# The place of eight scatter DMAs on the GpSimd queue of a two-layer transformer kernel

## The reference

```python
x = L0_attn_x                                    # (8, 256, 256)
h = _layernorm(x) * (1 + ca) + sa
x = x + ga * _L0_attn_ref(h, ...)                # 16 heads, causal softmax
h = _layernorm(x) * (1 + cb) + sb
x = x + gb * _L0_ffn_ref(h, ...)                 # 8 experts, top 2, and a shared one
h = _layernorm(x) * (1 + ca) + sa                # the second layer's ca, sa, ...
x = x + ga * _L1_attn_ref(h, ...)                # linear attention with a memory
h = _layernorm(x) * (1 + cb) + sb
x = x + gb * _L1_ffn_ref(h, ...)                 # 16 experts, top 4

# _L1_ffn_ref
t = xf * rsqrt(mean(xf * xf) + EPS) * norm_w
vals, idx = top_k(t @ gate_w.T + gate_b, 4)
G = zeros((M, E)).at[arange(M)[:, None], idx].set(softmax(vals))
h = einsum('mh,eoh->emo', t, w1) + b1[:, None, :]
act = a * sigmoid(ALPHA * a) * (b + 1.0)         # a, b: even and odd rows of h, clipped
y = einsum('emi,edi->emd', act, w2) + b2[:, None, :]
delta = einsum('me,emd->md', G, y)
return x + delta
```

## Time and profile before

| | |
|---|---|
| median of 3 runs | 1023.02 us |
| lowest, highest | 1021.14, 1023.75 us |
| the profiled execution's own time | 1023.02 us |
| its span, first to last instruction | 1021.0 us |
| busy: PE, DVE, ACT, POOL | 971.4, 715.6, 673.2, 426.9 us |
| mean granted TensorE clock | 0.984 |

### The profile page before, as it was taken

How to read it: one execution, slowest core, us unless ns; L and a number is a source line. 1 busy time by engine, 2 the same in 40 slices (tenths; PEclk the granted TensorE clock), 3 DMA queues, 4 the chain that set the end, 5 groups by cost and what they waited for, 6 DMA issues and landing times.

```text
span 1021.0 us, 20557 instructions
## 1 busy us (share of the span) xinstructions
PE 971.4 (95%) x6068; PEld 820.3 (80%) x6074; DVE 715.6 (70%) x2498; ACT 673.2 (66%) x1944; POOL 426.9 (42%) x445
## 2 busy tenths in 40 slices
PE   8999999999999999999999999999898799999990
PEld 5669878987977887888888788887677589999990
DVE  4464657766777677778777757784887678888880
ACT  3657768578668667857766866794746366777750
POOL 2322422331362254146145316424166556556563
PEclk9999999999999999999999999999999899999995
DMA  9926992999599220021021004337167799989964
GB/s 317 306 85 225 377 376 98 318 377 348 196 336 376 104 85 33 1 95 44 1 81 58 1 2 167 96 141 255 27 168 184 202 250 221 230 215 217 234 146 82
DMA packets 94380, 180.52 MB, mean 177 GB/s; under 512 B 9965, under 2 KB 29101, under 8 KB 93757
## 3 DMA queue, kind: packets, MB, share of 16 engines
q1 hardware_dynamic: 74459, 148.85, 43.9%
q0 software_dynamic: 18464, 30.01, 12.8%
q10 hardware_dynamic: 1346, 0.36, 0.2%
HBM read 77.42 MB, written 107.99 MB: 182 GB/s over the span
## 4 chain that ended last, share of the span: by engine, by line
PE 85%; DMA 4%; DVE 4%; issue 2%; POOL 2%; SPq 1%; ACT 1%; DVEq 0%; ACTq 0%; POOLq 0%
PE bank L1163 12%; PE bank L1129 11%; PE bank L1101 10%; PE bank L1184 6%; PE bank L1119 5%; PE bank L1091 5%; PE bank L1080 4%; PE bank L1050 3%; PE bank L1090 3%; PE bank L1120 3%; PE bank L1110 3%; PE bank L959 2%; PE bank L950 2%; PE bank L1032 2%; DMA RA<-in_L_attn_Wo 2%
## 5 line engine op out<-in xcount | busy, mean ns | idle before, releaser
L1978 POOL TENSOR_TENSOR RB<-RB 128x512 f32<-128x512 f32 x64 | 67.0, 1047 | 259.9 <-DVE RB L1764 259.7
L1163 PE MATMUL bank<-RB 128*128 128x128 f32 x1264 | 158.1, 277 | 2.8 <-DVE BC L1874 0.7
L1163 PEld LDWEIGHTS bank<-RB 128*128 128x128 f32 x1264 | 150.3, 193 | 6.2 <-ACT RB L1453 1.5
L1446 ACT ACTIVATE RB<-RA,nw 128x512 f32 x158 | 105.5, 714 | 48.4 <-issue 25.7
L1129 PE MATMUL bank<-RA,RB 128*128 128x256 f32 x512 | 133.0, 382 | 2.0 <-ACT RB L1347 2.0
L1101 PE MATMUL bank<-RA 128*128 128x256 f32 x512 | 121.3, 380 | 0.0
L1101 PEld LDWEIGHTS bank<-RA 128*128 128x128 f32 x512 | 95.0, 190 | 15.0 <-issue 3.3
L1129 PEld LDWEIGHTS bank<-RA,RB 128*128 128x128 f32 x512 | 91.2, 190 | 15.9 <-issue 3.0
L1954 POOL TENSOR_TENSOR qs<-qs,half 128x4 f32<-128x4 f32 x64 | 65.7, 1027 | 62.4 <-DVE qs L1773 49.3
L1184 PE MATMUL bank<-RB,BC 128*128 128x256 f32 x316 | 83.6, 388 | 1.7 <-DVE BC L1887 1.3
L1347 ACT ACTIVATE RB<-bank 128x256 f32<-128x256 f32 x128 | 48.6, 380 | 47.8 <-PE bank L1120 46.7
(11 more groups left out here) (253 smaller groups left out, 2383.2 us busy)
## 6 DMA issues: line engine op xcount, KB each, us to landing
xsD<-BC SPq DMA_DIRECT2D x17, 4232.0 KB, 32.9
RB<-in_w2b SPq DMA_DIRECT2D x79, 256.0 KB
RB<-xsD SPq DMA_DIRECT2D x61, 264.5 KB, 3.7
BC<-modD SPq DMA_DIRECT2D x16, 512.0 KB, 3.8
RA<-in_w SPq DMA_DIRECT2D x10, 512.0 KB
X<-xsD SPq DMA_DIRECT2D x18, 264.5 KB
RA<-in_L_attn_Wq SPq DMA_DIRECT2D x2, 1024.0 KB, 12.0
RA<-in_L_attn_Wo SPq DMA_DIRECT2D x1, 2048.0 KB, 18.5
```

Of the source, the lines that this page charges most:

```text
L1163: m = pe.matmul(ps[:, 128 * j:128 * j + 128], WS[:, n % 2, c, 128 * j:128 * j + 128], XT[:, n % 2, c * 128:c * 128 + 128], start=(c == 0), ...
L1446: m = act.activation(WS[:, n % 2, c, :], W1[:, bass.ds(r, 1), c, :].rearrange("p a n -> p (a n)"), ACT.Copy, scale=nw[:, c:c + 1])
L1978: pool.tensor_tensor(sq, qrow, qrow, ALU.mult).then_inc(mine("q_sq", p), 1)
```

## The change

The table `SENDS` and the method `put_behind` go. In their place stands a method `spread`, called with four `f_send` of sequence 6 and four numbers. It takes them out of the list and puts each behind a POOL stage counted from the last other `f_send` of sequence 6. The sequence 5's sends are in no call any more, and stay where the planner puts them.

```diff
-    def put_behind(self, moves):
-        for k, anchor in moves:
+    def spread(self, keys, every):
+        for k in keys:
             self.order.remove(k)
-            self.order.insert(self.order.index(anchor) + 1, k)
+        pool = [i for i, (stage, *key) in enumerate(self.order) if ENGINE[stage][0] == "POOL" and self.engine({"do": (stage, *key)}) == "POOL"]
+        last = max(i for i in pool if self.order[i][0] == "f_send" and self.order[i][2] == keys[0][2])
+        behind = [i for i in pool if i > last]
+        for n, k in reversed(list(enumerate(keys))):
+            self.order.insert(behind[every[n]] + 1, k)
...
-    (("f_send", 1, 5, 0, 3), ("ln_rs", 2, 6)),
...
-    (("f_send", 1, 5, 1, 3), ("f_send", 1, 5, 1, 2)),
-)
+SPREAD = 0, 1, 4, 5
...
-    p.put_behind(SENDS)
+    p.spread([("f_send", 1, 6, i, k) for i, k in ((1, 0), (1, 1), (1, 2), (1, 3))], SPREAD)
```

More of the change, by code:

```diff
@@ L192, in do @@
     return {"do": (stage, *key), **how}
[L195 to L199, removed]
-    (("f_send", 1, 5, 0, 3), ("ln_rs", 2, 6)),
-    (("f_send", 1, 5, 1, 0), ("f_gain", 5)),
-    (("f_send", 1, 5, 1, 1), ("f_x", 5)),
-    (("f_send", 1, 5, 1, 2), ("ln_rs", 1, 7)),
-    (("f_send", 1, 5, 1, 3), ("f_send", 1, 5, 1, 2)),
-)
+SPREAD = 0, 1, 4, 5
 W1_PARTS = (
```

## The result

The changed kernel took 1026.16 us (median of 19 runs, 1022.88 to 1029.08), the kernel before in the same sessions 1020.79 (19 runs, 1019.24 to 1023.75). The ratio is 1.0052, with a 95% interval of 1.0043 to 1.0060: slower by 5.4 us, where 1023.0 and no difference were forecast, and outside the range.

What follows compares the result with a forecast made beforehand. PE was taken as the bound, busy 971.4 of 1021.0 us. Terms 0 + 0 + 0 on the profiled execution's 1023.02 us gave 1023.0, range 1020.8 to 1025.6.

Steps and rivals of the forecast that it cites:

- The sends' pace: POOL, sequence 5: sends follow each other every 1.27 us, up to 1.36 beside DVE; last before `ln_rs(2, 6)` ends at 695.90.
- The step costs nothing as long as PE's earlier work covers it: Four more sends before `ln_rs(2, 6)` end it 1.53 us later, but PE's transposes still get data in time: cost 0.
- The term that the sum put at nothing: Cost of moving four sends ahead of `ln_rs(2, 6)` on POOL: taken as 0, upper end 0.6 us.
- the 0.6 taken as upper end: If each of the four sends took 1.54 us, data would reach PE at 698.85, 0.60 us late.
- the 0.48 us of cover: Slack left between `ln_x(2, 6)` data reaching PE at 697.77 and PE's transposes (L939) starting at 698.25.
- The port: Rival: the port shared with DVE holds sends from 692.4 on; transposes late 1.7 to 2.3 us, 1024.7 to 1025.3; chance 0.06.
- the full engines: Rival: full DMA engines hold the four sends; PE's data 6.7 us late, time 1029.7; chance 0.04.
- `f_gain(5)`, `f_x(5)`, the last weight loads: On POOL 1.5 and 0.4 us later; SP waits for both, but last weight loads still leave near 703.6: cost 0.
- the 2.6 us of cover on SP: SP's slack after `store(5)`, ending about 700.6, before the last two weight loads go out from 703.59.
- The sends that leave: Later sequence 5 sends on POOL, at 709.54, 711.08 and behind `f_x(5)`, go: gain taken as 0, bound 0.63 us.
- 0.06 for slower: Chance of slower beyond 0.3% (3.07 us): 0.04 for full engines, 0.02 for a port holding longer than priced.
- theory B: From the experiments, not the forecast: a long unbroken row of indirect sends on POOL keeps PE's completions from DVE and ACT.

Runs made afterwards that it cites:

- the first two experiments: Changed kernel with three weight loads held until sequence 5's sends landed: 1028.15 us, ratio 1.0056; changed kernel with those sends cut to 16 numbers a row: 1026.62 us, 1.0040.
- the run with six powers: Kernel before, sends in old places, with six small powers on POOL between the third send and `ln_rs(2, 6)`: 1025.03 us, ratio 1.0021.

## Why the prediction was wrong

**The sends' pace: right.** Seven at 1.26 to 1.28 us steps; the last ended at 694.84, 695.87 in before's time, against 695.90 forecast.

**"The step costs nothing as long as PE's earlier work covers it": this step failed.** It priced the sends only by how late they make POOL, and took it that PE, DVE and ACT go on meanwhile. On a chip with the stall they don't: from about 5 us behind the first send (691.25 against 686.17; by 3.4 us in sequence 7's row of before, 801.87 against 798.47), what PE has finished isn't taken up by DVE and ACT, which stand idle 3.75 and 4.15 us. The term that the sum put at nothing is 3.25 us of idle PE and 1.5 us for the clock at 0.50, 4.75 of the 5.0 us between the spans. The lateness itself, on the chip without the stall, is worth 0.77 us of idle time, beyond the 0.6 taken as upper end; the 0.48 us of cover counted on an `ln_x` of 0.74.

**The port and the full engines.** Both have the right sign and neither the mechanism. Sends never stood still; the first two experiments take the loads and the data away and the stall stays. The evidence against them was sequence 7's train, read for the pace of the sends alone. Its neighbours on ACT, DVE and PE in the same 10 us held the stall: 4.62, 3.61 and 4.60 us of idle time in the very rows' time. That one omission made a 5 us loss look like no change.

**`f_gain(5)`, `f_x(5)`, the last weight loads: not tested as priced.** Everything moved with PE: `bc(1, 7)` to 700.16, `store(5)` to 701.33, the last loads to 707.24 instead of 703.59. With 1.03 of shift the loads are 4.68 late, as much as PE; the 2.6 us of cover on SP held.

**The sends that leave: right.** No gain shows.

**The chances.** 0.06 for slower was too little for an order that had one example of itself in the trace, unread.

What stays open: by what means the row delays completions. The matmuls' starts are on time and the consumers are late, and the trace can't say whether the results or their news come late. The Trainium skill, "Perfetto Trace Analysis" (section "Tensor Engine Instruction (MATMUL, LD_WEIGHTS)"), says that TensorE's end in a profile is an estimate, and that the acknowledgement from PSUM and the update of the semaphore come behind it. That fits ends of 691.25 and 691.89 with consumers at 694.68 and 696.09, and no row here sees the step between. Open too: why one of three chips has no stall, how long a row may be (DVE was late by 0.84 us in a row of three, by 0.71 and 2.29 in rows of four), and the 2 us of the run with six powers. That theory B is the cause is shown by the length of the row, by the pauses and by the move to sequence 3; that it is the indirect form, only together with its longer time on POOL.

## What to carry to other kernels

Where a change makes a pattern longer that the kernel already has somewhere, read all engines at that place of the trace, not only the one that runs the pattern; a wait for "remote" on a core that shares with no other is something to explain first. Keep rows of indirect DMAs on POOL short beside TensorE work: here rows of two and three, with 1 us between, no longer made PE stand still for its results. Put other work of POOL between them that waits for nothing, even useless work, but not ahead of a step that PE waits for. Compare on more than one chip before believing "no difference".

## What the runs showed that I had not expected

- A row of seven indirect DMAs of 128 rows leaves DVE and ACT idle for 3.7 and 4.2 us in front of TensorE's results, whatever the bytes (16 or 529 numbers a row: 4.17 and 4.15 us on ACT). Five: 2.6 and 1.6. Three: none, but for a result that came only after the row. A pause of 2 us, or two of 1 us, shortens it so far that PE no longer waits for it.
- It showed on two chips and in the first traces, and never on the third: sequence 3's row cost 0.49% on one and 0.07% (interval with 0) on another.
- The last wait of the stall ends 1.2 to 1.6 us behind the end of the row's last send (ACT at sequence 5: 1.22 and 1.25; DVE at sequence 3: 542.23 against 540.66).
- A plain DMA of the same bytes holds POOL for 0.56 us (3.92 for seven), an indirect one for 1.27.
- Behind 3.25 us without work, TensorE's granted clock was 0.50 for the next 3 us.
- DVE's pair of `TENSOR_SCALAR` took 0.74 us beside a send, and in other traces 2.48 or 2.95, ending 0.15 us behind POOL's own arithmetic (with five sends 1.54, ending 0.50 behind it).
